# The last batch's norms and turned rows move from VectorE to ScalarE, and the table that deals the tail's steps to tiles is written anew

## What is computed

```
mod = (_silu(c) @ wmod).reshape(4, 6, 1, -1)        # sa, ca, ga, sb, cb, gb
h = _layernorm(x) * (1 + ca) + sa
x = x + ga * attention(h)
h = _layernorm(x) * (1 + cb) + sb
x = x + gb * ffn(h)

def ffn(x):
    expert = argmax(feats @ centroids.T, axis=1)
    alpha = sigmoid(sum(feats * centroids[expert]))
    n = layernorm(feats) * gamma[e] + beta[e]        # for the row's expert e
    y = feats + relu(n @ W1[e].T + b1[e]) @ W2[e].T + b2[e]
    return alpha * y + (1 - alpha) * feats
```

## Time and profile before

| | us |
|---|---|
| median of 3 runs | 809.66 (809.44 to 812.22) |
| profiled execution, its own time | 811.99 |
| its span, first to last instruction | 810.2 |
| TensorE busy in the span | 693.0 (86%) |
| VectorE | 545.7 (67%) |
| ScalarE | 503.0 (62%) |
| GpSimd | 259.3 (32%) |

### The profile page before, as it was taken

One profiled execution on the slowest core, in us unless ns is written; L12 is line 12 of the kernel. 1 busy time (PEld: TensorE's weight loads), 2 busy tenths in 40 slices (PEclk: granted clock), 3 DMA queues, 4 the chain that ended last, 5 costly groups with the idle time before them and its releaser, 6 DMA issues.

```text
span 810.2 us, 17292 instructions
## 1 busy us (share of the span) xinstructions
PE 693.0 (86%) x5199; PEld 344.7 (43%) x5199; DVE 545.7 (67%) x1249; ACT 503.0 (62%) x1182; POOL 259.3 (32%) x342
## 2 busy tenths in 40 slices
PE   4467999999999999978999998799798889897594
PEld 2252434334334434423344343244343225886594
DVE  6959667787856777745568767478587611798352
ACT  1440677676688767745877676466576578657372
POOL 2028129000214724330156253200344100456543
PEclk9866799999999999978999999799899799999898
DMA  8995914193260708260516093526123353533510
GB/s 226 320 177 216 157 32 133 55 186 76 51 118 2 234 4 157 44 189 29 94 26 210 3 157 60 173 52 121 33 100 100 111 181 96 162 94 118 178 57 10
DMA packets 54723, 92.04 MB, mean 114 GB/s; under 512 B 10161, under 2 KB 26061, under 8 KB 54120
## 3 DMA queue, kind: packets, MB, share of 16 engines
q1 hardware_dynamic: 48444, 79.72, 39.4%
q0 software_dynamic: 3520, 8.42, 3.1%
q10 hardware_dynamic: 2668, 2.78, 1.2%
HBM read 51.04 MB, written 37.90 MB: 110 GB/s over the span
## 4 chain that ended last, share of the span: by engine, by line
PE 55%; DVE 18%; issue 10%; ACT 8%; DMA 4%; another core or an unknown queue 2%; POOL 1%; DVEq 1%; ACTq 1%; SPq 0%; POOLq 0%
PE PS L1248 14%; PE PS L1208 13%; PE PS L1274 13%; ACT arenaA L1030 5%; DVE PS L1694 4%; PE PS L1325 3%; PE PS L1336 3%; DVE block_max L1701 3%; PE PS L1278 2%; DVE arenaA L1371 2%; DVE arenaB L1371 2%; ACT arenaB L948 2%; PE PS L1213 2%; DMA arenaB<-r_den 1%
## 5 line engine op out<-in xcount | busy, mean ns | idle before, releaser
L1030 ACT ACTIVATE arenaA<-PS 128x512 f32<-128x512 f32 (+3 forms) x768 | 333.1, 495 | 188.3 <-PE PS L1278 127.3
L1694 DVE CUSTOM_DVE_ANT_0 PS<-PS,mask 128x1024 f32<-128x1024 f32 (+3 forms) x256 | 261.7, 1035 | 119.0 <-PE PS L1208 104.8
L1274 PE MATMUL PS<-arenaA 99*128 99x512 bf16 (+3 forms) x768 | 228.9, 342 | 30.7 <-ACT arenaA L1030 18.7
L1208 PE MATMUL PS<-arenaA 96*128 96x512 bf16 (+3 forms) x768 | 207.5, 347 | 30.3 <-DVE block_max L1701 10.0
L1274 PEld LDWEIGHTS PS<-arenaA 99*128 99x128 bf16 x768 | 73.2, 99 | 223.7 <-ACT arenaA L1030 143.7
L1248 PE MATMUL PS<-arenaA,Vs 128*9 128x512 f32 (+3 forms) x1536 | 161.1, 496 | 0.0
L1701 DVE TENSOR_REDUCE block_max<-PS 128x8 f32<-128x1024 f32 (+1 forms) x96 | 100.4, 1046 | 37.6 <-PE PS L1213 30.5
L1208 PEld LDWEIGHTS PS<-arenaA 96*128 96x128 bf16 x768 | 68.6, 102 | 99.9 <-DVE maxima L1694 30.5
L1278 PE MATMUL PS<-after,identb 128*128 128x128 bf16 x512 | 105.7, 224 | 0.0
L842 POOL DMA_INDIRECT out_dram<-arenaA x46 | 46.7, 1016 | 103.2 <-DVE arenaA L1371 94.8
L1079 ACT ACTIVATE arenaA<-PS,b1p 128x128 f32<-128x128 f32 x184 | 52.7, 373 | 34.5 <-PE PS L1325 20.1
(11 more groups left out here) (219 smaller groups left out, 687.8 us busy)
## 6 DMA issues: line engine op xcount, KB each, us to landing
arenaA<-k_parts SPq DMA_DIRECT2D x96, 128.0 KB, 8.2
arenaA<-by_expert SPq DMA_DIRECT2D x46, 192.5 KB, 3.7
o_raw<-OT SPq DMA_DIRECT2D x32, 256.0 KB, 3.3
k_parts<-arenaB SPq DMA_DIRECT2D x24, 256.0 KB, 3.8
arenaA<-q_parts SPq DMA_DIRECT2D x16, 384.0 KB, 4.9
q_parts<-arenaB SPq DMA_DIRECT2D x18, 256.0 KB, 3.7
arenaA<-in_L_ffn_W_dram SPq DMA_DIRECT2D x2, 2048.0 KB, 13.2
arenaA<-q_parts SPq DMA_DIRECT2D x16, 256.0 KB, 5.7
```

The costliest lines, as they stand in the source:

```text
L1030: a.activation(PT[:, u % EB, h, off:HALF], PS[:, 4 + n % SB_, off:HALF], ACT.Exp).then_inc(exp_ok, 1)
L1208: last = mm(PS[:, place + c0 // HALF, at:at + c1 - c0], SQ(g, h)[0:KROWS, t * P:(t + 1) * P], SK(g, h)[0:KROWS, c0:c1], start=(at == 0), s ...
L1274: last = mm(bank[:, off:HALF], SK(g, h)[0:MROWS, kb * P:(kb + 1) * P], SQ(g, h)[0:MROWS, qc * HALF + off:(qc + 1) * HALF], start=True, sto ...
L1694: v.tensor_tensor_reduce(out=src, in0=src, in1=mask[:, S - n:S], scale=1.0, scalar=-3e38, op0=ALU.add, op1=ALU.max, accum_out=maxima[:, pl ...
```

## The change

ScalarE gets the last batch's eight norms of x and eight norms of h (`last_norm`) and the two copies of H0 and H1. It computes scale x + bias, so VectorE makes a bias row (`bias_x`, `bias_h`, one instruction on 128x8 each) in place of the norms. `scale_h` now waits for ScalarE (`x_normed`). The hand-written tables move the steps from H on one tile earlier on TensorE, GpSimd's pieces and the table one tile earlier, the end of `root_h` from tile 22 to tile 19, and put two root steps where the norms were. The bank for S is freed by ScalarE.

```diff
-        R_AT = {6: ("O0", "O1"), 15: ("H0", "H1"), 17: ("S",), 19: ("C",)}
-        ACT_AT = {18: "sigmoid"}
-        POOL_AT = {15: 0, 16: 1, 17: 2, 18: 3, 19: 4, 20: 5, 22: 6}
+        R_AT = {6: ("O0", "O1"), 14: ("H0", "H1"), 16: ("S",), 18: ("C",)}
+        ACT_AT = {13: ("norm_x0",), 14: ("norm_x1",), 16: ("H0", "H1"), 18: ("sigmoid",), 21: ("norm_h0",), 22: ("norm_h1",)}
+        POOL_AT = {14: 0, 15: 1, 16: 2, 17: 3, 18: 4, 19: 5, 21: 6}
...
-            spread("root_h", 10, 20, 3) + ((22, "norm_h0"), (23, "norm_h1")) + tuple((23 + (n + 1) // 2, "table") for n in range(5))
+            tuple((22 + (n + 1) // 2, "table") for n in range(5))
...
+            def last_norm(step):
+
+                act.wait_ge(post_chain, (AT_BIAS_X if step[5] == "x" else AT_BIAS_H) + 1)
+                dst, src = (h_tile, x_tile(B - 1)) if step[5] == "x" else (row_tile, h_tile)
+                half = int(step[6])
+                for t in range(half * 4, half * 4 + 4):
+                    last = a.activation(dst(t), src(t), ACT.Identity, bias=ln2[:, 8, t:t + 1], scale=ln2[:, 7, t:t + 1])
+                if half:
+                    last.then_inc(x_normed if step[5] == "x" else pay_ok, 1)
...
-                step = ACT_AT.get(n)
-                if step == "sigmoid":
-                    sigmoid(B - 1)
+                for step in ACT_AT.get(n, ()):
+                    if step == "sigmoid":
+                        sigmoid(B - 1)
+                    elif step in TAIL_ACT:
+                        k = POST.index(step)
+                        evacuated(B - 1, "R", step, TAIL_BANKS[k][0], N_END + k, ACT_END + TAIL_ACT.index(step) + 1)
+                    else:
+                        last_norm(step)
...
-                elif step in ("norm_x0", "norm_x1"):
-                    linked(AT_NORM_X)
-                    last = half_norm(b, h_tile, x_tile(b), int(step[-1]))
-                    last.then_inc(post_chain, 1)
+                elif step in ("bias_x", "bias_h"):
+                    linked(AT_BIAS_X if step == "bias_x" else AT_BIAS_H)
+                    v.scalar_tensor_tensor(L2(8), L2(0), -1.0, L2(7), ALU.mult, ALU.mult).then_inc(post_chain, 1)
                 elif step == "scale_h":
-                    linked(AT_SCALE)
+                    dve.wait_ge(x_normed, B)
                     tt(H2, H2, over(b, 2), ALU.mult).then_inc(post_chain, 1)
...
-                elif step in ("norm_h0", "norm_h1"):
-                    linked(AT_NORM_H)
-                    half_norm(b, row_tile, h_tile, int(step[-1])).then_inc(pay_ok if step[-1] == "1" else post_chain, 1)
```

More of the change, by code:

```diff
@@ L324, in build @@
         FIRST_BANKS = banks([(kind, k) for kind, _, k in FIRST])
-        TAIL_BANKS = ((0, None), (1, None), (0, 0), (1, 1), (0, 2), (0, 4))
+        TAIL_BANKS = ((0, None), (1, None), (0, "O0"), (1, "O1"), (0, "H0"), (0, "S"))
+        TAIL_DVE, TAIL_ACT = ("O0", "O1", "S", "C"), ("H0", "H1")
+        ACT_END = ACT_PER["first"] + (B - 2) * ACT_PER["middle"] + ACT_PER["last"]
         CLAMPED = "the table holds sums of flags and rows that a minimum keeps inside the regions"
@@ L1294, in tail @@
             def tail(k):
-                bank, before = TAIL_BANKS[k]
-                maximum("R", 0, POST[k], (N_END_DVE + MB_ + (0 if before is None else before + 1), None), bank, B - 1, 0)
+                bank, freed_by = TAIL_BANKS[k]
+                by_dve = 0 if freed_by is None else TAIL_DVE.index(freed_by) + 1 if freed_by in TAIL_DVE else None
+                by_act = TAIL_ACT.index(freed_by) + 1 if freed_by in TAIL_ACT else None
+                maximum("R", 0, POST[k], (None if by_dve is None else N_END_DVE + MB_ + by_dve, None if by_act is None else ACT_END + by_act),
+                        bank, B - 1, 0)
             pe.wait_ge(w_back, 32)
@@ L1503, in half_stats @@
                     last.then_inc(post_chain if isinstance(b, int) and b == B - 1 else done, 1)
-            def half_norm(b, dst, src, half):
-                for t in range(half * 4, half * 4 + 4):
-                    last = v.tensor_scalar(dst(t), src(t), ln2[:, 0, t:t + 1], ln2[:, 7, t:t + 1], ALU.subtract, ALU.mult)
-                return last
             def only_dve(b, step):
```

21 lines of the change are left out of this document (11 added, 10 removed).

## The result

The changed kernel took 816.14 us (median of 9 runs, 812.69 to 818.2), the kernel before beside it 810.29 (9 runs, 807.47 to 813.95): ratio 1.0068, 95% interval 1.0044 to 1.0093. **Slower by 0.7%**, where 807.6 us and a range up to 811.9 were forecast. The profiled execution took 818.2 us with a span of 816.4 (before: 811.99 and 810.2). The last tile's second product ends at 804.54, before at 798.40; what comes behind is as long as before. So all 6.1 us lie ahead of it.

What follows compares the result with a forecast made beforehand. TensorE's pace of 1.88 us a tile after the freeze was taken to set the end. The freeze ending sooner, less one tile, gave -2.5 to -1.1; -2.1 off the median 809.66 made 807.6 us, range 804.6 to 811.9.

Steps and rivals of the forecast that it cites:

- What bounds the kernel now: Tail: the end is the quiet stretch's end, 761.6, 4.9 us to tile 28, then 17 tiles at 1.88 us: 798.4.
- rival C: Tail: no freeze or a short one, the load of tile 31 gates; -7.1 us, 802.6 us; chance 0.13.
- x half: Norms of x: VectorE stands 2.5 us at scale_h, tile 16's copy 2.6 us later, S at 724.9, 0.3 us gained.
- Routing: From S to tile 20: ScalarE's wait before the sigmoid shrinks to some 2.8 us; tile 20 ends at 736.8, 1.3 late.
- rival E: Scatters not sooner: VectorE's small steps stretch under GpSimd's sums, bias_h at 740; +1.5, 811.2 us; chance 0.07.
- rival D: Tail: ScalarE and table together, half clock for three tiles, three stores queued; slower, 814.2 us; chance 0.09.
- h half: Norms of h: bias_h at 737.1, pay_ok at 741.9, first scatter 742.7 against 745.87, 3.2 us sooner.
- The sum: Tail: the freeze ends at 757.2, tile 27 done 4.9 later, 18 tiles follow: 795.9 against 798.4; -2.1 us taken.
- rival B: Tail: the table's last steps, behind tile 24 on VectorE, are caught by the freeze; +1.3, 811.0 us; chance 0.25.
- A: The forecast itself: the freeze ends sooner with one tile fewer done, -2.1 us, 807.6 us; chance 0.46.
- the freeze: Beside back-to-back scatters: TensorE's results seen late from about 3 us after the first scatter until 10.0 to 15.8 after it.
- The rule of the Trainium skill: VectorE: offloading it when saturated makes the 5.8 us taken off the gain, 803.9 us; not taken by the forecast.

Runs made afterwards that it cites:

- before_again: The kernel before, unchanged, run again on chip 13 for its trace: 782.62 us (one run).
- after_again: The changed kernel, unchanged, run again on chip 13: 780.94 us, ratio 0.9972 to the kernel before.
- table_early: The changed kernel with the five steps of the last table two tiles sooner on VectorE, chip 13: 782.12 us, ratio 0.9983 to the kernel before.
- old_places_hold: old_places with TensorE held ahead of tile 27's first product until tile 24's store has landed, chip 10: 791.55 us, ratio 1.0103 to the kernel before.
- old_places: The changed kernel with every chain step from scale_h on back at its tile in the kernel before, chip 13: 780.51 us, ratio 0.9975 to the kernel before.
- h_only: old_places with the eight norms of x back on VectorE, chip 13: 781.04 us, ratio 0.9968 to the kernel before.
- before_hold: The kernel before with TensorE held ahead of tile 28's first product until tile 25's store has landed, chip 11: 788.13 us, ratio 1.0058 to the kernel before.
- after_hold: The changed kernel with TensorE held ahead of tile 26's first product until tile 23's store has landed, chip 11: 790.67 us, ratio 1.0090 to the kernel before.

## Why the prediction was wrong

**What bounds the kernel now** was half right. Rows, waits and their coincidence with scatters were read correctly, and the waits came again in the changed kernel (4.66 and 6.30 us on VectorE, 12.13 on ScalarE, until 761.4; forecast by 759). The cause was argued from three coincidences and fell: before_again has the same scatters and no waits. As it was taken as a property of the kernel, only rival C, at 0.13, allowed for its absence.

**x half**: right in mechanism. scale_h at 715.22 after 2.14 us of waiting (716.5 and 2.5 forecast), copy of tile 16 at 716.36, H at 719.62, S at 724.90 (724.9 forecast). This execution's tiles began 1.2 us sooner than those of before (tile 8 ended at 702.27, before at 703.49); counted from there scale_h and the copy are right within 0.1, H is 0.8 and S 1.2 late. That is the clock behind the wait: the step costed tile 16's first product, tile 14's second and H at 1.06 us each, they took 1.42, 1.92 and 1.65.

**Routing**: the step that failed first. ScalarE's wait ahead of the sigmoid was 2.93 us (2.8 forecast), but tile 20 ended at 741.77 and not at 736.8, counted from tile 8 it was 6.2 late: 1.2 from S; 1.7 from the half clock in 727 to 731; 2.4 from the wait ahead of tile 22, where, for the most part beside GpSimd's sums, four small steps of VectorE took 0.58 to 0.83 us and not 0.2, and the two additions of a tile's finish 1.32 and not 0.62 (the trace of the kernel before has such rows too, 0.80 at 731.71 and 1.51 at 736.00, and the forecast passed them over); 1.6 from the half clock behind that wait. (Those are 6.9; C's own wait, for which 1.5 stood in the sum, was short.) The forecast had the stretching only in rival E, and the half clock only in rival D and only behind the freeze.

**h half**: forecast bias_h 737.1, norms done 741.9, first scatter 742.7; measured 739.72, 744.64, 746.82. Late by 2.6, 2.7 and 4.1: ScalarE's share was sized rightly, 4.9 us, and everything was late when it began. The last 1.4 is GpSimd, which had to do tile 21's store first. On chip 13, in the execution without half clock (after_again), the first scatter was 1.6 us sooner than before's, half of the 3.2 forecast; in table_early, with it, 2.3 us later.

**The sum and rival B**: the table. The prediction gave the catch 0.25, and D 0.09, with tile 24 seen only after 757 as the deciding point. It was seen at 761.49. From the end of the wait to tile 28 the first chip's traces have 4.8 before and 11.1 after, 6.3 apart; two tiles fewer (3.9) and the table (2.2), as priced in one trace each of the hand-made waits, make 6.1. With the wait's own end 1.0 later, and 1.2 off for the sooner start, that is the 6.1 us of the profile. The agreement is no proof: the medians didn't confirm the 2.2, and old_places_hold didn't fit. D's price, 814.2, was 1.9 short, and its terms were not those of the trace: it had three queued stores and half clock on three tiles behind the freeze, where the trace has two stores, half clock on two tiles, and half clock ahead of the scatters. B's own sum was wrong as well: 19 tiles at 1.88 behind 762.7 to 763.6 end at 798.4 to 799.3, not at 799.2 to 800.5. The direction was wrong because A and B were worked out with tiles 23 to 25 done in time, and no term stood for their being late: when the first scatter began, the changed kernel had computed two tiles fewer than the kernel before (tile 22 was done, before tile 24), and from there the freeze did the rest.

**The rule of the Trainium skill** that was weighed, offloading a saturated VectorE, would have given 803.9. No run has it: with and without the norms of x on ScalarE the time is the same (old_places 780.51, h_only 781.04). **C**, no freeze, was given 0.13 and would make the change 7.1 us faster. A chip without the freeze exists, and there it is 2.2: the kernel before is rid of it too (its tile 28 ends 60.7 and not 63.0 after tile 8). The page of the Trainium skill that C leaned on (Trainium Architecture — The Big Picture, What this means for kernel authors: lanes and DMA ports can't contend) isn't decided by it: the traces from the four later chips agree, those from the first have the waits, and whether they are contention no run shows.

## What stays open

What makes the waits on the first chip. What was shown is that they are absent on chip 13 with the same instructions, and that a wait put in by hand, at the tiles where the first traces have it, turns the sign. A cause that nobody tested is the recording of the profile itself. The two first traces hold 9968 and 9984 semaphore events, the eighteen others 11145 to 11190, for the same work; up to the first scatters the numbers nearly agree (3183 against 3197 in before_again, between 100 and 340 us in the kernel before), and the events are missing behind that. Something between the engines and the record was disturbed when the scatters began. Whether this and the waits have one cause, and whether the kernel would wait without the profiler, no run tells.

The hand-made wait reproduces 2.5 of the 5.9 us in the medians. In the profiled executions it is 5.3 of 6.1, but that pair flatters it: before_hold's is 1.1 us under its median, after_hold's 1.8 over. The rest may be half clock, of which the changed kernel's nine runs on the first chip have more (mean clock 0.933 in the median, before 0.939 in its one profile; on chip 13 0.958 and 0.957), but this was not separated. Nor do I know what brings the clock down: the same wait of 2.70 us has it behind it in one execution and not in another, on one chip.

## What to carry to other kernels

Look for the event that sets the end (here mostly the last scatter: the end follows it by 39 to 43 us in every trace without a long wait) and cost each edit by what it does to that event; work taken off a busy engine for its own sake was worth nothing measurable here (the norms of x). Where work moves to earlier places in a table, ask how many tiles are done in time when the known wait begins, and keep what a later load needs, the table here, clear of it. And take a profile again elsewhere before costing a wait for which it names no releaser: the same two kernels stood at 1.0068 on the first chip and at 0.9972 on chip 13.

## Not expected of the hardware

The same kernel takes 27 us (3.4%) longer on the first chip than on the four others, which agree within 0.6 us, and the difference is not spread over it. The two traces of the kernel before are less than 1 us apart for the first 340 us; then 10, 9, 7 and 2 us are lost at the four rows of scatters, and less than 1 us anywhere else. The first chip has single waits of up to 12 us of VectorE and ScalarE on TensorE's results there, the others none. And one piece of code, tile 8 to tile 20, took 34.8 and 39.2 us in two executions on one chip (after_again and table_early on chip 13), with the granted clock at full all the way in the one and at half three times in the other.
